# Pairs of masked half steps: both transposed energies first, then both mask products, in a four-layer attention kernel

## The reference, cut to what matters

```python
scores = jnp.einsum('bhqd,bhkd->bhqk', Q, K) / np.float32(np.sqrt(DK))
if mask is not None:
    scores = jnp.where(mask[:, None, :, :] == 0, jnp.float32(-1e+20), scores)
A = jax.nn.softmax(scores, axis=-1)
out = jnp.einsum('bhqk,bhkd->bhqd', A, V).transpose(0, 2, 1, 3).reshape(b, sq, D)
return out @ wo + bo
```

## Time and profile before

| | |
|---|---|
| median of three runs | 2722.91 us (2715.34 to 2726.97) |
| the profiled execution | 2719.28 us, its span 2717.3 us |
| mean granted clock of PE | 0.956 of full speed |
| busy: PE, DVE, ACT, POOL | 2500.1, 1783.6, 1381.5, 739.8 us |
| masked stages a2, a3 | from 658 to 1257 us of the span |
| masked stages a4, a5 | from 1753 to 2352 us of the span |

### The profile page before, as it was taken

One profiled execution on the slowest core, in us unless ns is written; L12 is line 12 of the kernel. 1 busy time (PEld: TensorE's weight loads), 2 busy tenths in 40 slices (PEclk: granted clock), 3 DMA queues, 4 the chain that ended last, 5 costly groups with the idle time before them and its releaser, 6 DMA issues. The chain is left out here.

```text
span 2717.3 us, 44289 instructions
## 1 busy us (share of the span) xinstructions
PE 2500.1 (92%) x16014; PEld 1373.0 (51%) x16014; DVE 1783.6 (66%) x4364; ACT 1381.5 (51%) x1921; POOL 739.8 (27%) x867
## 2 busy tenths in 40 slices
PE   6999999988999999997999997799999999797896
PEld 3544433333444444443999997334434444385553
DVE  3566777777677777774457774577777777455554
ACT  1544455544555555555357875255555555452332
POOL 2243335433321110201016564102222112223012
PEclk7999999989999999998899999699999999998998
DMA  6222222122133223220127785422322322001331
GB/s 177 53 50 71 58 61 65 37 54 61 43 96 94 70 75 92 78 53 25 40 86 217 221 221 130 115 71 78 108 61 73 91 73 60 9 1 42 83 85 41
DMA packets 102212, 218.54 MB, mean 80 GB/s; under 512 B 19116, under 2 KB 35372, under 8 KB 100716
## 3 DMA queue, kind: packets, MB, share of 16 engines
q1 hardware_dynamic: 93164, 203.66, 27.5%
q0 software_dynamic: 8832, 12.06, 2.4%
HBM read 100.34 MB, written 12.58 MB: 42 GB/s over the span
## 5 line engine op out<-in xcount | busy, mean ns | idle before, releaser
L1120 ACT ACTIVATE probT_a<-scores 128x1024 f32<-128x1024 f32 (+3 forms) x832 | 779.0, 947 | 712.5 <-PE scores L951 420.6
L1228 DVE CUSTOM_DVE_ANT_0 ring<-ring,maskb_a 128x512 f32<-128x512 f32 x1024 | 686.3, 716 | 172.9 <-PE ring L969 163.6
L969 PE MATMUL ring<-stacks_a 64*128 64x512 f32 (+7 forms) x1664 | 468.2, 461 | 53.3 <-DVE negm_a L1226 17.3
L990 PE MATMUL outputs<-probT_a,V_a 128*32 128x512 f32 (+6 forms) x3328 | 443.9, 576 | 12.5 <-ACT oT_a L1129 8.5
L1226 DVE TENSOR_REDUCE negm_a<-ring 128x1 f32<-128x512 f32 (+3 forms) x640 | 332.1, 563 | 139.7 <-PE ring L975 105.4
L930 PE MATMUL scores<-stacks_a 64*128 64x512 f32 (+7 forms) x1664 | 399.7, 449 | 2.4 <-DMA stacks_a<-narrow_a 2.4
L969 PEld LDWEIGHTS ring<-stacks_a 64*128 64x128 f32 (+1 forms) x1664 | 211.7, 190 | 376.0 <-issue 140.2
L930 PEld LDWEIGHTS scores<-stacks_a 64*128 64x128 f32 (+1 forms) x1664 | 170.7, 187 | 249.6 <-issue 151.9
L889 POOL TENSOR_SCALAR maskb_a<-ints_a 128x1024 bf16<-128x1024 int32 x31 | 112.8, 3639 | 423.5 <-DMA ints_a<-in_mask 353.4
L899 POOL TENSOR_TENSOR ve<-mv,epsilon 128x1 f32<-128x1 f32 x96 | 18.2, 190 | 725.0 <-DVE mv L1195 725.0
L951 PE MATMUL scores<-maskT_a,identb 64*64 64x512 bf16 x1024 | 211.0, 402 | 0.0
(11 more groups left out here) (240 smaller groups left out, 3741.0 us busy)
## 6 DMA issues: line engine op xcount, KB each, us to landing
stacks_a<-parts_a SPq DMA_DIRECT2D x672, 128.0 KB
raw<-in_moew SPq DMA_DIRECT2D x92, 512.0 KB, 3.9
ints_a<-in_mask SPq DMA_DIRECT2D x31, 512.0 KB, 3.7
swapped_a<-maskT_a SPq DMA_DIRECT2D x32, 256.0 KB, 3.7
wt<-in_w SPq DMA_DIRECT2D x7, 1024.0 KB, 4.9
kvT_a<-in_ctxT SPq DMA_DIRECT2D x12, 512.0 KB, 3.4
wrow<-in_row SPq DMA_DIRECT2D x7, 512.0 KB, 5.9
stacks_a<-narrow_a SPq DMA_DIRECT2D x224, 8.0 KB
```

Source lines behind the costliest of these rows:

```text
L969: last = pe.matmul(bank("S", j, n, e)[:, 0:w], Q[rows, g, qt * P:(qt + 1) * P], K[rows, g, 0:w], start=True, stop=not a.causal)
L990: last = pe.matmul(OB[x * slot:(x + 1) * slot, q0:S], V[:, m % 2, kb, c:c + slot], probT[:, kb % 2, x, q0:S], start=(kb == 0), stop=(kb == ...
L1120: act.activation(probT[:, kb % 2, 2 * p:2 * p + 2, q0:S], scores_bank(j, n)[:, :, q0:S], ACT.Exp, bias=0.0, scale=-1.0).then_inc(c_exp.sem, 1)
L1228: least = dve.tensor_tensor_reduce(sc, sc, maskb[:, m % 2, qt, :], 1.0, BIG * 2, ALU.add, ALU.min, out)
```

## The change

Only the generator of the order is changed, and only for masked half steps. An even one now yields S, its own ST, the ST of the odd one after it, its own mask products and exponential, then those of the odd one, then its work beside. The odd one yields its S, its work beside and PV. The numbers of instructions do not change.

```diff
         for h in range(halves):
-            kinds = (("ST", "S", "exp") if not reorder else ("ST", "exp", "S") if h % couples else ("S", "ST", "exp"))
-            for kind in kinds:
+            if not reorder:
+                turns = (("ST", h), ("S", h), ("exp", h))
+            elif h % couples:
+                turns = (("S", h),)
+            else:
+                turns = (("S", h), ("ST", h), ("ST", h + 1), ("exp", h), ("exp", h + 1))
+            for kind, n in turns:
                 if kind == "S" and there(j + 2):
-                    yield (kind, j + 2, h)
+                    yield (kind, j + 2, n)
                 if kind != "S" and there(j):
-                    yield (kind, j, h)
+                    yield (kind, j, n)
```

## The result

The changed kernel takes 2865.23 us in the median of 3 runs (2863.57 to 2867.56) against 2722.91: a ratio of 1.0517 (95%: 1.0491 to 1.0543). Timed again on another occasion it was 2866.07 against 2724.53 (1.0514, 1.05 to 1.0528). The forecast was 2870, in a range from 2800 to 2930. The profiled execution took 2863.57 us, with a span of 2861.6. On the second occasion one of the six executions took 3771.35 us, at a mean granted clock of 0.551; the ratio leaves it out.

The account below looks back on a forecast made before the run. PE was taken to bound the masked stages, with ACT's copies coming late after the change. Terms 77 + 22 + 37 - 17 = +119, plus 32 for the clock, +151 on 2719.28, gave 2870 us, range 2800 to 2930.

Parts of the forecast that it names:

- first pairs of a unit: Half steps 2 and 3: products with V wait for ACT's copy behind two exponentials, +1.2 us each, 64 times, +77 us.
- q or k in an even half step: Chain through ACT and DVE stays but starts later in the pair: +0.57 us in 38 pairs, +22 us.
- other even half steps with work: ot, V, mask transposes, x, read out by ACT: +0.53 us, middle of -0.20 and +1.26, in 70 pairs, +37 us.
- all others: 84 pairs with nothing beside, or only in the odd half step: 0.20 us saved each, -17 us.
- clock: PE's waits in first pairs drop the granted clock 21 times at 1.5 us each: +32 us, 0 to 109.
- plain pair: Pair without work beside: PE's steps take 3.00 us instead of 3.20, with second mask products at 0.23.
- Waits without falls: Rival: same waits on PE, but no stretch idle enough to lower the clock; 2838 us, chance 0.31.
- Clock falls in every first pair: Rival: all 64 first pairs lower the clock, 1.7 us each, 109 us; 2947 us, chance 0.08.
- The faster one: Rival: ACT's copies stay hidden and PE's saving shows in full, 256 x -0.20 = -51 us; 2668 us, chance 0.05.
- Hardly any change: Rival: all low ends at once, cheapest mask products and slack for copies and work; +18 us, 2737 us, chance 0.04.

Follow-up runs that it names:

- run 10: Changed kernel with the first product of S in half step 3 of masked units done five times, beside the changed kernel on one chip: 2839.04 us, 1.0423 of before.
- run 5: Changed kernel with the first product of S in half step 3 of masked units done five times, timed on an earlier occasion: 2832.69 us, 1.039 of before.
- Run 1: Changed kernel, but ACT alone walks its entries in the order of before; PE keeps the gathered order: 2750.49 us, 1.0084 of before.
- run 2: Changed kernel with only the copy of the outputs moved, to the end of half step 1, ahead of the gathered exponentials: 2795.56 us, 1.0237 of before.
- Run 3: Changed kernel with the work beside of even masked half steps put behind the odd one's S, on all engines: 2765.61 us, 1.0155 of before.
- run 9: Changed kernel, unchanged, timed and profiled again on the same chip as the kernel with the wait filled: 2866.07 us, 1.0514 of before.
- Run 7: Both moves on the changed kernel, but on, ot, y and last mask transpose with x keep their places, on ACT between the exponentials: 2702.4 us, 0.9909 of before.
- Run 6: Kernel before with copy of outputs at half step 1's end and even masked work behind the odd S, without the pairing: 2758.18 us, 1.0112 of before.
- run 4: Changed kernel with copy of outputs at half step 1's end and even masked work behind the odd one's S: 2709.88 us, 0.9936 of before.

## Why the prediction was right

**The sum, term by term.** The masked stages' pairs, in us more than before:

| term | predicted | changed kernel | wait filled (run 10) |
|---|---|---|---|
| first pairs of a unit (64) | +77 | +93.4 | +76.8 |
| q or k in an even half step (38) | +22 | +17.1 | +16.9 |
| other even half steps with work (70, here 73) | +37 | +34.5 | +30.8 |
| all others (84, here 79) | -17 | -11.2 | -10.9 |
| clock | +32 | in the rows above | mostly gone |
| sum | +151 | +133.9 | +113.6 |

*First pairs.* The step held as written: two exponentials, then the copy, then the products with V. 4.92 us where 5.0 was reckoned, since PE needs less ahead of the mask products. At full clock all three kinds lose the same 1.14 us, as the prediction had it: 3.78 to 4.92 alone, 4.73 to 5.87 with "on", 4.56 to 5.70 with a mask transpose (5.70 in run 5; in the changed kernel falls make it 6.26). 64 x 1.14 is 73; the rest of the 93.4 is mostly the clock. PE's waits list oT's copy 33 times, 1.43 us each (47.1 / 33), "on" 15 times at 1.8, S for the narrow copy 15 times at 1.5 (22.9 / 15): the places that the prediction named, close to its counts of 34, 15 and 14. Run 1 shows the cause on ACT, run 2 the copy's share.

*q and k.* 5.66 to 5.74 us where 5.77 was forecast. Run 3 shows that the loss goes when the work is moved behind the second S.

*Other even half steps.* The middle of the bounds, 0.53 each, was a choice; 0.47 came out. In it lie +1.06 for the pair with a mask transpose and x, +0.2 for one with y, ot and on, and +0.3 to +0.5 for the others. Run 1 takes it to +3.5 in all: ACT's order.

*All others.* The step was mis-sized in both directions. A plain pair saves 0.32, not 0.20: the second mask products cost 0.24, as taken (0.23), but S and both energies take 0.89 in place of 1.00 (880.02 - 879.13), as the two energies together take 0.56 and not 0.66, a step that no row of before showed. (The Trainium skill, "TensorEngine Tiling (Array Packing)", section "Key Properties", says that a change of tiling mode drains the engine, and gives no price; the pair that changes it less often is shorter here by these 0.32 us, which agrees. That the drain is all of it, no run shows.) Yet only 21 of the 79 show it in full. The 15 that open a batch, behind two pairs with q or k, save 0.07 (3.14 us), a cost that the prediction had not seen; run 3, which moves the work beside, returns it. Most of the 14 with V save 0.11. And 10 pairs at the ends of a3 and a5, where no S is left to do, take 5 us more together, mostly 2.88 each where it was 2.53: there PE waits for the exponential that read the same buffer of energies.

```profile
1323.03 0.49 PE L935 MATMUL scores<-stacks_a 64*128 64x512 f32 x2
1323.85 0.50 PE L935 MATMUL scores<-stacks_a 64*128 64x512 f32 x2 [0.33 <-ACT probT_a L1125]
```

The prediction asked whether these buffers come free in time only for pairs with an S in them. Even there little is left: in the plain pair above the second exponential ends at 893.01 and the second energies start at 893.15, by the single rows of the trace.

*The clock.* In the first profile, 84.5 us of the masked stages were at the lower level where before had 13.3, in 21 falls, the number forecast; 13 of them lie in the 29 first pairs that it was reckoned from, 8 elsewhere. At 0.40 per us that is 28 us, and in run 9's (104.7 against 7.0) 39, where 32 was forecast. The two rows at 898.91 and 902.32 show one: PE is busy 1.84 of 3.41 us at full clock, because S waits 1.57 us for ACT's narrow copy, and the next stretch has a granted clock of 0.50, that is 1.2 GHz. Shortly before 20 of the 21 falls stands a wait of PE of 1.1 to 1.9 us (worked out from the gaps in PE's rows), 11 of them of an S for a copy of ACT and 5 of "on". The Trainium skill ("TensorE: Matmul & The Clock Gate", section "HAM oscillation — how this bites in real kernels") warns of longer idle gaps; read as the prediction read it, that waits as short as these leave the clock up, it is not borne out. By that reading run 10 would have gained nothing; it gained 27 us in the median.

**What was luck.** The change is worth 133 us in the masked stages of the first profile and 141 in the second, not the 151 forecast. In the first profile a start that took 11 us more brought 2863.57 nearer to 2870. The number of falls was a guess, and came out as 21 in one profile and 25 in the next. Without the clock the waits are about 103 us (113.6, less 0.40 x 26.6 for the falls that run 10 kept), 16 below the 119 forecast; the clock's price, 28 and 39 by the same reckoning, lies on both sides of its 32.

**The rivals.** Waits without falls (2838) is ruled out by runs 9 and 10: it is near what the kernel takes with most of the falls gone, 2839. Clock falls in every first pair (2947) had 64 falls, and there are 21 to 25. The faster one asked for 1.26 us of slack at the copy of the outputs; in run 1, where ACT has only one exponential ahead of it, PE still waits for it. Run 7, which takes these waits away, is faster by 0.9%, not by 2%. Hardly any change (2737) needed all low ends at once, and the first pairs, q or k and the other work all came out well above theirs.

**What stays open.** Run 6's loss: its masked stages take 1229.9 us, 32 more than before. PE is idle 21 us longer there, waiting 43.2 us for DVE in place of 19.0, and busy 11 longer, with 33.6 us at the lower clock in place of 13.3; the other 14 us that PE is busy longer lie in the untouched start (116.1 us at the lower clock there, 78.5 before). Why DVE comes later, no run tells. Run 7 still does not collect 256 times 0.32 us: in a4 with a5 it gains nothing, and no run moved DVE's work there. And in both profiles of the changed kernel PE waits 78 times for 1.1 us or more in the masked stages, while the clock falls 21 and 25 times; which of these waits bring a fall is not shown.

## What to carry to other kernels

Steps that are gathered on one engine to save it switches are gathered on every engine that walks the same list. Before doing so, look at what the engine behind has queued after its part, here a short copy that now stands behind two long exponentials, and at how long the bottleneck can do without it: 0.15 us of slack was in the rows, and 1.26 were taken. Such copies can be put ahead of the long instructions; that alone left the kernel 2.4% slower here (run 2), and only with the other work moved too did a saving show, 0.6% (run 4) and 0.9% (run 7).

## What was not expected of the hardware

PE paid twice for waits of 1.1 to 1.9 us: 240 products that change nothing, put into them, made the kernel 27 us faster side by side (2866.07 to 2839.04), though a first pair without more beside still takes its 4.92 us. The number of falls of the clock is not a constant of the kernel: 21 and 25 for the same program with the same waits, and 78.5 to 112.6 us at the lower level in the untouched start of the changed kernel's two profiles. Two energies in a row take 0.56 us together (879.46 to 880.02), less than twice the 0.32 of one, although S, energies and energies all use the array in the same division (64*128 in the rows).
